# Tokens routed and sent to their experts in four groups beside attention's values, and the first bias moved into gelu

## What is computed

```python
x = x + conv_ref(group_norm(x))        # a small MLP learnt step by step over t, then read out
t = x.reshape(4, 1024, 128)
t = t + attention(layer_norm(t))       # additive attention in a band of 32 positions
t = t + ffn(layer_norm(t))             # 8 experts, each token goes to its best 2

# ffn, with xn the normalized token
weights, chosen = top_k(softmax(xn @ Wr + br), 2)      # weights made to sum to 1
h = gelu((xn * ln_g[e] + ln_b[e]) @ W1[e] + b1[e])     # 128 -> 512
y = h @ W2[e] + b2[e]                                  # 512 -> 128
out = sum(weights[k] * y[chosen[k]] for k in range(2))
```

## Time and profile before

| What | us |
|---|---|
| median of 3 runs (lowest, highest) | 1091.23 (1091.07, 1095.33) |
| the profiled execution's own time | 1092.72 |
| its span, first to last instruction | 1090.8 |
| busy: PE, DVE, ACT, POOL | 781.9, 697.0, 609.9, 571.0 |
| mean granted clock of PE (share of full speed) | 0.874 |

### The profile page before, as it was taken

How to read it: one execution, slowest core, us unless ns; L and a number is a source line. 1 busy time by engine, 2 the same in 40 slices (tenths; PEclk the granted TensorE clock), 3 DMA queues, 4 the chain that set the end, 5 groups by cost and what they waited for, 6 DMA issues and landing times. The chain is left out here.

```text
span 1090.8 us, 24858 instructions
## 1 busy us (share of the span) xinstructions
PE 781.9 (72%) x8328; PEld 497.3 (46%) x8328; DVE 697.0 (64%) x1667; ACT 609.9 (56%) x1287; POOL 571.0 (52%) x738
## 2 busy tenths in 40 slices
PE   2656888888888888888888697555680006999980
PEld 2345544545454545444444243204550005988970
DVE  0573688888888888888888626795853002555554
ACT  2444788888878888888888231682330003555540
POOL 0033577777777777777777593100006772545550
PEclk9775899999999999999999799786765557999995
DMA  9003920000000000000000320300001112222217
GB/s 209 0 1 70 122 1 0 0 0 0 0 0 0 0 0 0 0 0 0 0 0 0 78 78 0 96 1 0 4 1 39 51 54 55 74 72 70 71 52 238
DMA packets 58539, 39.22 MB, mean 36 GB/s; under 512 B 17904, under 2 KB 51336, under 8 KB 58496
## 3 DMA queue, kind: packets, MB, share of 16 engines
q1 hardware_dynamic: 52256, 28.53, 13.0%
q0 software_dynamic: 4544, 9.38, 2.5%
q10 hardware_dynamic: 1696, 0.72, 0.4%
HBM read 19.40 MB, written 16.66 MB: 33 GB/s over the span
## 5 line engine op out<-in xcount | busy, mean ns | idle before, releaser
L360 POOL TENSOR_TENSOR s_w<-l_kw,l_m 128x512 f32<-128x512 f32 x192 | 238.4, 1281 | 12.2 <-DVE l_m L511 12.2
L511 DVE SCALAR_TENSOR_TENSOR l_m<-l_m,l_eta,lp_g 128x256 f32<-128x256 f32 x512 | 219.6, 476 | 37.1 <-PE lp_g L623 25.9
L457 ACT ACTIVATE l_kw<-s_w,l_keep_lr 128x256 f32<-128x256 f32 x384 | 171.3, 507 | 0.0
L1254 ACT ACTIVATE f_hh<-fp_h 128x1024 f32<-128x1024 f32 x39 | 39.9, 1024 | 167.6 <-PE fp_h L1336 167.6
L1276 POOL DMA_INDIRECT f_yg<-f_yr,f_xmeta x78 | 74.9, 960 | 85.7 <-DVE f_yr L1494 73.5
L1271 POOL DMA_INDIRECT f_xg<-f_xrow,f_place x64 | 61.9, 967 | 64.1 <-DVE f_xrow L1451 44.9
L1486 DVE TENSOR_TENSOR f_hs_lo<-f_hh,f_hs_hi 128x1024 bf16<-128x1024 f32 x39 | 47.8, 1225 | 67.5 <-ACT f_hs_hi L1258 67.5
L1312 PE MATMUL fp_x<-f_identb,f_xt 128*128 128x128 bf16 x156 | 15.8, 226 | 94.7 <-DMA f_xt<-f_xg 94.6
L450 ACT COPY l_wt<-lp_b 128x512 f32<-128x512 f32 x96 | 56.4, 588 | 27.8 <-PE lp_b L616 27.8
L1475 DVE COPY f_xf<-fp_x 128x512 bf16<-128x512 bf16 x39 | 16.2, 416 | 81.0 <-PE fp_x L1312 80.9
L365 POOL TENSOR_TENSOR l_kw<-s_w,l_keep 128x512 f32<-128x512 f32 x64 | 65.2, 1039 | 0.1
(11 more groups left out here) (309 smaller groups left out, 2110.0 us busy)
## 6 DMA issues: line engine op xcount, KB each, us to landing
f_xt<-f_xg SPq DMA_DIRECT2D x39, 130.0 KB, 2.2
f_xg<-s_pad SPq DMA_DIRECT2D x1, 4992.0 KB, 32.9
s_w<-f_yg SPq DMA_DIRECT2D x16, 256.0 KB, 4.1
xs<-in_x_dram SPq DMA_DIRECT2D x4, 512.0 KB, 9.5
s_w1r<-in_L_ffn_W_dram SPq DMA_DIRECT2D x8, 256.0 KB, 2.8
r_w<-in_L_ffn_W_dram SPq DMA_DIRECT2D x8, 256.0 KB, 3.5
out_dram<-s_x SPq DMA_DIRECT2D x8, 256.0 KB, 3.3
t_xsh<-t_xl SPq DMA_DIRECT2D x4, 448.0 KB, 3.5
```

What stands on the lines that cost most here:

```text
L360: nc.gpsimd.tensor_tensor(W[k][:, half(h), :], KW[k][:, half(h), :], M[k][:, half(h), :], ALU.add).then_inc(w_ready[k], 1)
L457: m = nc.scalar.mul(KW[k][:, b, :], W[k][:, b, :], keep_lr[:, b:b + 1])
L511: i = nc.vector.scalar_tensor_tensor(out=M[k][:, b, :], in0=M[k][:, b, :], scalar=eta[:, b:b + 1], in1=ps_g[b][:, 0:256], op0=ALU.mult, op ...
```

## The change

Values of attention move from `attend` into `experts` and are interleaved there with routing in four groups g of eight tiles (two values of n, four batches). Each group is normalized, routed, counted and placed on its own, and its 16 sends follow at once. This is possible because every expert has a region of 4096 slots of its own in `xg` (with 7 x 256 rows more, 34560 in all), so that a place needs only the counts so far (`carry`). The 39 tiles are numbered by owner as before; where tile j starts is a table, `start_i`, from which SP loads a register before each transfer. The root of the second layer norm is taken by another formula, with one ACT instruction per group for both roots. Per group ACT takes a root and an exponential; `second` copies the whole rows, 256 bf16 columns of eight tiles.

The product of ln_b and W1 moves into read-out (in rounds 3, 4, 6 and 8 on PE), with `w1` in four buffers instead of eight; the bias table's eight DVE instructions go into its last four rounds, and its six small loads to SP there. The constants `lim` and `job` are made on POOL at the end of read-out. In `experts` PE turns table and owners into one bias column per tile and block (`bcol`), gelu adds it, and the four bias products of L1334 are gone; those of L1346 stay. Gelu runs per block of 256 columns, cast and remainder per half of 512, and PE signals after each half.

In the cut below `masked(n)`, `valued(n)`, `weights(n)` and `values(n)` are the old lines L1117 to L1121, L1124 to L1136, L1058 to L1063 and L1066 to L1074, with one buffer of `at1` and `at2` instead of two; `spread(g)` is three small instructions on the variances, `remainder(g)` is L1380 for eight tiles, `routed(g)` is L1399 to L1441 on 64 columns with `carry` added to the slots, `counts(g)` L1303 and L1304, `features(g)` the two copies of turned tokens.

```diff
@@ read_out: sync, gpsimd, tensor, vector
+                    if e == 4:
+                        for i in range(3):
+                            sp.dma_start(b1r[E * i:E * i + E, :], inp["L1_ffn_b1"]).then_inc(b_in, 16)
+                            sp.dma_start(bb[E * i:E * i + E, H:H + 128], inp["L1_ffn_b2"]).then_inc(b_in, 16)
                     if e >= 4:
                         sp.wait_ge(w_lo, 2 * (e - 3))
-                    sp.dma_start(sb["w1r"][:, e, :], inp["L1_ffn_W1"][e]).then_inc(load_w[e % 4], 16)
+                        sp.wait_ge(hb_done, e - 3)
+                    sp.dma_start(w1[e % 4][:, :], inp["L1_ffn_W1"][e]).then_inc(load_w[e % 4], 16)
...
+                nc.gpsimd.iota(limi[:, :, :], [[B * S, E], [256, 16]], base=0, channel_multiplier=0).then_inc(counted, 1)
+                nc.gpsimd.iota(jobi[:, :], [[256, 2 * B * S // 256 + E - 1]], base=0, channel_multiplier=0).then_inc(counted, 1)
+                pool.wait_ge(counted, 2)
+                nc.gpsimd.tensor_copy(sb["lim"][:, :, :], limi[:, :, :]).then_inc(counted, 1)
+                nc.gpsimd.tensor_copy(sb["job"][:, :], jobi[:, :]).then_inc(counted, 1)
...
+                    if k in (3, 4, 6, 8):
+                        for e in range(2 * (3, 4, 6, 8).index(k), 2 * (3, 4, 6, 8).index(k) + 2):
+                            pe.wait_ge(cleared, 7)
+                            pe.wait_ge(load_w[e % 4], 32 * (e // 4 + 1))
+                            nc.tensor.matmul(ps_b[0:NSPLIT, 0:H], lnb3[:, NSPLIT * e:NSPLIT * e + NSPLIT], w1[e % 4][:, :],
+                                             start=e == 0, stop=e == E - 1).then_inc(hb_done, 1)
...
+                        return nc.vector.tensor_tensor(bb[:, 0:H], ps_b[0:NSPLIT, 0:H], b1r[:, :], ALU.add)
...
+                    if k >= N + 1:
+                        for i in range(2 * (k - N - 1), 2 * (k - N - 1) + 2):
+                            if i >= 1:
+                                dve.wait_ge(tab, i)
+                            bias(i).then_inc(tab, 1)
...
@@ experts: sync, scalar
+                    first = nc.sync.value_load(start_i[0:1, j:j + 1], min_val=0, max_val=E * REGION + SL * (E - 2))
+                    sp.dma_start(tile[j % RING][:, :, :], sb["xg"][bass.ds(first, SL), :].rearrange("(a p) c -> p a c", p=128)).then_inc(xt_in[j % RING], 16)
...
+                def turned_weights(n):
+                    act.wait_ge(at_done, n + 1)
+                    if n >= 1:
+                        act.wait_ge(v_done, n)
+                    nc.scalar.copy(at1[:, :], ps_am)
+                    nc.scalar.copy(at2[:, :], ps_tail).then_inc(at_ready, 1)
...
+                def roots(g):
+                    act.wait_ge(nrm, 4 * g + 3)
+                    nc.scalar.activation(sr[:, :, :], sq[:, :, :], ACT.Sqrt).then_inc(sq_ready, 1)
...
+                def second(g):
+                    act.wait_ge(x_lo, g + 1)
+                    nc.scalar.copy(of_group(row[1][:, :, 0:128].bitcast(BF16), g), of_group(row[0][:, :, 0:128].bitcast(BF16), g)).then_inc(x_dup, 1)
+
+                def odds(g):
+                    act.wait_ge(gap_ready, g + 1)
+                    nc.scalar.activation(p2[:, :], p2[:, :], ACT.Exp).then_inc(ex_ready, 1)
+
+                turned_weights(0)
+                turned_weights(1)
+                for g in range(GR):
+                    if 2 * g + 2 < NTB:
+                        turned_weights(2 * g + 2)
+                    roots(g)
+                    rows(g)
+                    features(g)
+                    if 2 * g + 3 < NTB:
+                        turned_weights(2 * g + 3)
+                    second(g)
+                    odds(g)
+                act.wait_ge(owner_ready, 4)
                 for j in range(NJ):
-                    act.wait_ge(h_done, j + 1)
                     if j >= 2:
-                        act.wait_ge(h_lo, j - 1)
-                    nc.scalar.activation(hh[j % 2][:, :, :].rearrange("p h n -> p (h n)"), ps_h[j % 2][:, :], ACT.Gelu).then_inc(h_ready, 1)
-                    act.wait_ge(h_ready, j + 1)
+                        act.wait_ge(h_lo, 2 * (j - 1))
+                    for h in range(NH):
+                        if h % 2 == 0:
+                            act.wait_ge(h_done, 2 * j + h // 2 + 1)
+                        nc.scalar.activation(hh[j % 2][:, h, :], ps_h[j % 2][:, SL * h:SL * h + SL], ACT.Gelu,
+                                             bias=bcol[:, h, j:j + 1]).then_inc(h_ready, 1)
                     if j >= 2:
                         act.wait_ge(y_done, j - 1)
-                    nc.scalar.copy(hs[j % 2][0][:, :, :], hh[j % 2][:, :, :]).then_inc(h_hi, 1)
+                    for p in range(2):
+                        act.wait_ge(h_ready, NH * j + 2 * p + 2)
+                        nc.scalar.copy(hs[j % 2][0][:, 2 * p:2 * p + 2, :], hh[j % 2][:, 2 * p:2 * p + 2, :]).then_inc(h_hi, 1)
...
@@ experts: gpsimd, tensor
+                for g in range(GR):
+                    pool.wait_ge(place_ready, 2 * g + 2)
+                    pool.wait_ge(meta_ready, 2 + 2 * g + 2)
+                    pool.wait_ge(x_lo, g + 1)
+                    pool.wait_ge(x_dup, g + 1)
+                    for i in range(GT):
+                        for k in range(2):
+                            nc.gpsimd.indirect_dma_start(sb["xg"][:, :], bass.IndirectOffsetOnAxis(ap=place[:, g, k, i:i + 1], axis=0),
+                                                         row[k][:, tile_of(g, i), :], None).then_inc(sent, 16)
...
+                def router(g):
+                    pe.wait_ge(xn_ready, GT * (g + 1))
+                    if g == 0:
+                        pe.wait_ge(load, 32)
+                    for j in range(2):
+                        pe.wait_ge(xnf_ready, 2 * g + j)
+                        for b in range(B):
+                            m = nc.tensor.transpose(ps_xn[:, 128 * b:128 * b + 128], xn[g % 2][:, B * j + b, :], ident)
                         m.then_inc(xn_turned, 1)
-                    if g >= 1:
-                        pe.wait_ge(xnf_ready, g)
-                        for n in range(4 * g - 4, 4 * g):
-                            m = nc.tensor.matmul(ps_r[:, E * n:E * n + E], xnf[:, 128 * n:128 * n + 128], wr[:, :], start=True, stop=True)
-                m.then_inc(lg_done, 1)
-
-                for e in range(E):
-                    m = nc.tensor.matmul(ps_b, lnb3[:, NSPLIT * e:NSPLIT * e + NSPLIT], sb["w1r"][:, e, :], start=e == 0, stop=e == E - 1)
-                m.then_inc(hb_done, 1)
-                pe.wait_ge(count_ready, 1)
-                pe.wait_ge(id_ready, 2)
-                flat = both[:, :, :].rearrange("p e n -> p (e n)")
-                nc.tensor.matmul(ps_c, sb["cst"][:, C_LOW:C_LOW + 128], flat, start=True, stop=True).then_inc(count_done, 1)
-                nc.tensor.matmul(ps_k, ones[:, :], flat, start=True, stop=True).then_inc(count_done, 1)
+                    for j in range(2):
+                        pe.wait_ge(xnf_ready, 2 * g + j + 1)
+                        for b in range(B):
+                            i = B * j + b
+                            m = nc.tensor.matmul(ps_r[:, E * i:E * i + E], xnf[j][:, 128 * b:128 * b + 128], wr[:, :], start=True, stop=True)
+                        m.then_inc(lg_done, 1)
...
+                for n in range(2):
+                    weights(n)
+                    values(n)
+                for g in range(GR):
+                    if 2 * g + 2 < NTB:
+                        weights(2 * g + 2)
+                        values(2 * g + 2)
+                    router(g)
+                    if 2 * g + 3 < NTB:
+                        weights(2 * g + 3)
+                        values(2 * g + 3)
+                    counts(g)
...
-                            nc.tensor.matmul(p, btab[:, 128 * h:128 * h + 128], mine[:, j:j + 1].to_broadcast([128, SL]), start=True, stop=False)
-                            for i, (a, c) in enumerate(PRODUCTS):
-                                m = nc.tensor.matmul(p, chosen(w1s[a], e, h), xf[j % 2][:, c, :], start=False, stop=i == 2)
-                        m.then_inc(h_done, 1)
+                            for r, (b, c) in enumerate(PRODUCTS):
+                                m = nc.tensor.matmul(p, chosen(w1s[b], e, h), xf[j % 2][:, c, :], start=r == 0, stop=r == 2)
+                            if h % 2 == 1:
+                                m.then_inc(h_done, 1)
...
@@ experts: vector
+                def normed(g):
+
+                    dve.wait_ge(sq_ready, g + 1)
+                    nc.vector.reciprocal(rd[:, :, :], sr[:, :, :]).then_inc(nrm, 1)
+                    dve.wait_ge(nrm, 4 * g + 4)
+                    if g >= 2:
+                        dve.wait_ge(xn_turned, 2 * g - 2)
+                        dve.wait_ge(x_hi, g - 1)
+                        dve.wait_ge(x_lo, g - 1)
+                    for i in range(GT):
+                        t = tile_of(g, i)
```

(36 more changed lines are left out.)

441 lines of the change are left out of this document (208 added, 233 removed).

## The result

The changed kernel takes 1068.8 us (median of 4 runs, 1067.46 to 1070.44) where the kernel before takes 1093.24: ratio 0.978 [0.976, 0.9795]. It is faster, by 24.4 us instead of the 40 forecast, and outside the range. The profiled execution took 1068.27 us, of which the span is 1066.4.

What follows compares the result with a forecast made beforehand. POOL's sends, then PE's 39 tiles were taken to bound the kernel, each stage wholly on the path. 1092.7 + 7 + 4 (read-out) - 34 (sends) - 16.7 (loop) - 0.7 (loop's start, first and last tiles) = 1052 us; range 1044 to 1067.

Steps and rivals of the forecast that it cites:

- The two stages on the path: Before: POOL's 64 sends alone, 824 to 909 us, then PE's 39 tiles, 909 to 1057 us, one resource each.
- Part 1: Learning loop: the slow fill of the larger region takes about 150 us instead of 43.2, hidden; cost 0, at most 1.
- Part 2: Read-out: eight bias products on PE add 7 us, eight small DVE instructions add 4 us.
- Part 3: Routing: sends in groups beside it, last send ending at 871 instead of 905.1 on the old time axis, -34 us.
- Part 4: Expert loop: four of sixteen up products go, -0.43 us per tile if PE stays the bound, 39 tiles, -16.7 us.
- The ring through gelu: Expert loop: up products' end through gelu, cast, remainder to down products; with halves 3.2 us against PE's 3.35, 0.15 spare.
- both limits agree today: Old expert loop, period 3.78 us: PE's products and the gelu, cast and remainder chain equally long; shortening PE alone gains nothing.
- A: Expert loop: gelu, cast and remainder bind, period 3.6, gain 7 us instead of 16.7; 1062 us, chance 0.14.
- B: Routing: groups slower, 27 us each, by waits at hand-overs among five engines; last send 883, 1064 us, chance 0.14.
- C: Routing: POOL binds, DVE ahead, clock high; last send at 865, 1046 us, chance 0.10.
- E: Routing: grouped sends still start after the last group, leaving the loop's gain less read-out's cost; 1086 us, chance 0.02.
- D: Routing: lock between DVE and sends, each send waiting out a DVE instruction, 2.3 us per send; 1113 us, chance 0.03.

Runs made afterwards that it cites:

- the combined kernel: Changed kernel with one load of the expert's number per tile, routing's exponential ahead of the rows' copy, gelu's table loaded before the loop: 1047.67 us, ratio 0.9584.

## Why the prediction was right and wrong

**What bounds it.** The two stages on the path were the right ones. That each had one resource was wrong of the loop: a PE busy 146.55 of 148 us was the array nearly filled by a stream that was itself a little longer.

**Part 1, pad rows: right.** Over the page the large fill lands 107.2 us after its issue and the slow one 147.2. PE's busy time from 116 to 600 us is 416.87, before 416.98: the learning loop doesn't feel them.

**Part 2, read-out: right.** +11 forecast, and 1 for the block change and three small instructions; the mask work begins 11.6 us later (761.80 against 750.18), and read-out's own stretch grew by as much (69.1 to 80.8 us). In another execution of the same kernel it begins at 763.94, so the meeting of the two numbers is good to some 2 us.

**Part 3, sends: right.** First send 794.57 (forecast 795), last 878.03, so that it ends at 878.99, 3 us before the forecast's 882. The places of the first three groups are ready 22.5 us apart (23), those of the last after 19.2. The last two groups run without a gap, and the sends cost 0.977 us in the mean. They were not "all alike" before: 958 ns is the median of the earlier trace rows and 1332 the longest. The order of the waits within a group was only partly right: root's table load (797.15 to 798.43), which I had put off the path, is on it, and the exponential's wait was worth next to nothing (0.2 us in the combined kernel), since the counts were as late. PE's clock was granted 0.50 from 795 to 880 us, as in the routing rows that its durations were taken from (0.50 from 785 to 790 us before). Both hide in a term that came out right as a sum. The exponential's switch of tables cost its row of 1.28 us and nothing ahead of it: the load starts 0.02 us after the copy of 2048 columns (809.14 + 1.91 to 811.07) and its instruction begins at 812.36.

**Part 4, loop: wrong, the whole miss.** The step that failed is "-0.43 us if PE stays the bound, 39 x 0.43 = -16.7 us". It took PE's time for the array's, and the sentence "PE has the same load of the owner before its products and no gap there" passed over the reason: the gap wasn't there because sixteen up products on the array covered the sequencer's work. Twelve don't. A product that goes takes 0.11 us off the array, but off the stream only some 0.02 (the stretch from the first up product's weight load to the next load of the owner, 1.01 us, became 0.92 for four products fewer), and the address work that had run beside the bias product now stands bare, with no product beside it, ahead of the first up product (from the load of the owner to the first up product's weight load 0.82, now 0.87; all four are medians over 32 tiles). In its place the runs showed a third limit, the stream: 3.77 us per tile before and 3.79 after, whatever the array saves. With it relieved on both sides, the forecast's 0.43 is there: 3.68 to 3.23, 0.45 per tile. The ring through gelu was no trap: with one load it holds 3.23. That "both limits agree today" was seen, of two limits out of three; and the 0.2 us from the remainder's end (988.63) to the down products was the sequencer's as well, whose rows of the owner's load end only at 988.66 in that tile.
The start of the loop came 0.9 us later behind the last send (13.2 us to the first down products, now 14.1; forecast 0.3: SP's load with its register work is 0.26 + 0.15), and gelu's table load, which the forecast didn't have, is on the path: it lasts 1.28, and without it the stretch is 0.8 shorter.

```profile
L1225 SPq TENSOR_LOAD <-f_starti x39: 262/268/476, 880.4 to 1016.9; - x39
```

**Sum.** Without Part 4's 16.7 us the sum reads 1092.7 + 7 + 4 - 34 - 0.7 = 1069; measured 1068.3. That they meet so well is partly luck: on the old axis the sends end 37.7 us earlier (905.09 against 878.99 - 11.6), not 34, and the loop's start and its first and last tiles gave nothing back, where 0.7 was forecast.

**Rivals.** The miss landed just beyond A (1062) and B (1064) with neither's mechanism. C and E did not happen. D did not either, at its price: the sends take 0.977 us in the mean, before 61.88/64 = 0.967. But its lock is there, and the prediction's case against it was misread. The send at 986.98 ran across the remainder of 987.40 because it had begun first. A send that begins while DVE is in an instruction with both inputs in SBUF ends 0.83 us after that instruction; one that begins in an instruction with an input in PSUM (`fp_v`) is not held up. One of each kind, DVE's line first:

```profile
803.16 1.19 DVE L1495 TENSOR_TENSOR f_xrow<-f_xn,f_xrow 128x1024 bf16<-128x1024 f32 x1
803.75 1.43 POOL L1313 DMA_INDIRECT f_xg<-f_xrow,f_place  x1 [0.30 <-issue]
...
817.39 0.68 DVE L1457 TENSOR_TENSOR s_x<-fp_v,s_x 128x512 f32<-128x512 f32 x1
817.60 0.96 POOL L1313 DMA_INDIRECT f_xg<-f_xrow,f_place  x1 [0.31 <-issue]
```

Over all traces, of 214 sends that began inside such an instruction of the first kind over 0.4 us long (0.02 us or more from either of its ends), 204 waited for its end, and the other ten had begun within 0.1 us of its start; of 49 that began in one of the second kind none waited (none took over 0.97 us). Where the send began first, the traces show no wait of DVE (last section). It cost little here because only two of the 64 sends began in a long one: all sends together lost 1.3 us.

## What to carry to other kernels

Before taking an engine's busy share as its bound, add up the rows of its sequencer in one turn of the loop: loads of values, register operations, waits, and the 0.06 us between them. Here an "issue" row ahead of PE's products was the sign. With the stream at the period (3.79 us per tile) removing work from the array gained 0 to 3 us, and the cheap edit was to load a value once and keep it (21 us). Of two level limits (3.77 and 3.68 before) both had to be relieved: the loop part alone was worth 0 to 3 us, the single load alone (on before) 2.4, the two together 21.5 (1071.5 to 1049.99).

## What the runs showed of the hardware

- A load of one value from SBUF into a register of PE took 0.30 us, with 0.15 of register work and 0.02 of an assertion row (SEQ_ASSERT) behind it, 0.65 from its start to the sequencer's next row; on SP the load took 0.26. A third load cost the loop 0.74 us.
- One load fewer also halved the fused register operations of the tile (from ten to five, with twelve plain ones for eight), so that its register rows fell by 0.55 us where the load's own three are 0.47.
- An indirect send of POOL that began inside a DVE instruction with two inputs in SBUF waited for its end (204 of 214); begun ahead of it, in the changed kernel's loop, it took its usual 0.96 us, and the instruction was not held up either (remainders of 512 columns 0.68 to 0.72 us in all traces). With one load per tile and the rows in halves 22 to 27 of the loop's 78 result sends took over 1 us (up to 1.48; five traces, none of the two series below), since they began inside a remainder; in the changed kernel none did (959 ns in the mean). POOL was not the bound there.
- In two of the six series every kernel with the grouped routing lost 20 to 38 us in a way that the kernel before, run in turns with them, did not (1093.2 and 1094.3 us there). The same combined kernel took 1047.67, 1049.2 and 1086.19 us. In the last, waits for PE's products in the routing stage end 3 to 9 us after the products' own rows, and the profile names no releaser (DVE at the router's result, ACT at the turned weights):

```profile
813.67 0.22 DVE L1515 TENSOR_TENSOR f_lg<-fp_y,f_s 128x64 f32<-128x64 f32 x1 [8.19 <-remote]
```
```profile
818.61 0.59 ACT L1248 COPY f_at<-fp_y 128x512 f32<-128x512 f32 x1 [12.24 <-remote]
```

  The last send is at 900.3 instead of 878 to 880, and the loop runs at 3.70 us per tile instead of 3.24, at a granted clock of 1.00 in both. The granted clock in routing is 0.50 in both too. Whether this belongs to a chip or to a moment, why the kernel before is spared, and what the unaltered changed kernel would take there stays open; it was not run in them. Each of the six series had another chip, so the record can't part the two. It also means that kernels of different series should be compared only through a yardstick with the same stages.
